# A two-layer graph kernel on one core: layer 2's attention scores as 32-row by 64-column TensorE tiles, one head in each row group, in place of keys masked by head

## The reference, cut to what matters

```python
# layer 2 (L1 in the code): 12 heads of 32 features, scale = 384 ** -0.5
q = (x @ Wq.T).reshape(b, n, 12, 32)
k = (x @ Wk.T).reshape(b, n, 12, 32)
v = (x @ Wv.T + bv).reshape(b, n, 12, 32)
bias = (adj + adj)[:, None]
scores = einsum('bqhd,bkhd->bhqk', q, k) * scale + bias
...
p = softmax(scores, axis=-1)              # a row whose scores are all zero gives zero
out = einsum('bhqk,bkhd->bqhd', p, v).reshape(b, n, h)
return out @ Wo.T + bo
# then x = layernorm(x + layer 2's result)
```

## Time and profile before

| | |
|---|---|
| median of 3 runs | 2078.02 us (2076.94 to 2078.02) |
| profiled execution, its own time | 2075.99 us |
| its span, first to last instruction | 2074.2 us |
| PE busy | 1963.2 us, 95% of the span |
| DVE busy | 1396.7 us, 67% |
| ACT busy | 1129.7 us, 54% |
| mean granted TensorE clock | 0.981 of full speed |

### The profile page before, as it was taken

One profiled execution on the slowest core, in us unless ns is written; L12 is line 12 of the kernel. 1 busy time (PEld: TensorE's weight loads), 2 busy tenths in 40 slices (PEclk: granted clock), 3 DMA queues, 4 the chain that ended last, 5 costly groups with the idle time before them and its releaser, 6 DMA issues.

```text
span 2074.2 us, 46190 instructions
## 1 busy us (share of the span) xinstructions
PE 1963.2 (95%) x16192; PEld 1878.7 (91%) x16192; DVE 1396.7 (67%) x2622; ACT 1129.7 (54%) x2456; POOL 424.9 (20%) x555
## 2 busy tenths in 40 slices
PE   5499999999999999999999999997999999999997
PEld 5399999999999999999999999997899999999997
DVE  4466666766666666766667666654777767776775
ACT  4256555565455555565555654553556565556555
POOL 2111212211121111212122121221122212221221
PEclk8699999999999999999999999999999999999999
DMA  7434444443444444444444434334222222222221
GB/s 177 125 86 119 111 114 119 108 120 102 123 112 117 108 108 130 105 116 107 115 122 107 121 101 123 104 99 116 66 83 77 66 81 83 77 67 80 84 77 63
DMA packets 268787, 213.52 MB, mean 103 GB/s; under 512 B 142928, under 2 KB 251216, under 8 KB 268752
## 3 DMA queue, kind: packets, MB, share of 16 engines
q1 hardware_dynamic: 268752, 213.06, 38.5%
HBM read 120.34 MB, written 79.69 MB: 96 GB/s over the span
## 4 chain that ended last, share of the span: by engine, by line
PE 75%; ACT 9%; DVE 8%; issue 5%; DMA 2%; SPq 1%; ACTq 0%; POOL 0%; POOLq 0%; DVEq 0%
PE a_bank L384 41%; PE b_bank L1173 15%; PE b_banks L1173 5%; PE b_banks L1215 4%; PE a_bank L450 3%; PE b_bank L1238 2%; ACT a_work L626 2%; PE a_bank L435 2%; PE b_banks L1225 2%; ACT L626 2%; ACT L594 2%; ACT a_work L594 1%; DVE a_hid_lo L772 1%; PE b_bank L1248 1%; DVE a_ctxt_lo L757 1%
## 5 line engine op out<-in xcount | busy, mean ns | idle before, releaser
L384 PE MATMUL a_bank<-a_x1t_hi,a_w_hi 128*128 128x256 f32 x1152 | 327.0, 284 | 8.3 <-DVE a_x1t_lo L757 8.3
L384 PE MATMUL a_bank<-a_x1t_hi,a_w_lo 128*128 128x256 f32 x1152 | 323.7, 281 | 0.0
L384 PE MATMUL a_bank<-a_x1t_lo,a_w_hi 128*128 128x256 f32 x1152 | 323.4, 281 | 0.0
L626 ACT ACTIVATE a_work<-a_bank,a_b 128x256 f32<-128x256 f32 x384 | 159.3, 465 | 225.6 <-PE a_bank L384 225.1
L384 PE MATMUL a_bank<-a_w_lo,a_hid_hi 128*128 128x384 f32 x768 | 258.2, 336 | 0.0
L384 PE MATMUL a_bank<-a_w_hi,a_hid_lo 128*128 128x384 f32 x768 | 258.1, 336 | 0.0
L384 PE MATMUL a_bank<-a_w_hi,a_hid_hi 128*128 128x384 f32 x768 | 258.1, 336 | 0.0
L384 PEld LDWEIGHTS a_bank<-a_x1t_hi,a_w_hi 128*128 128x128 f32 x1152 | 218.9, 190 | 17.4 <-DVE a_x1t_lo L757 8.8
L384 PEld LDWEIGHTS a_bank<-a_x1t_lo,a_w_hi 128*128 128x128 f32 x1152 | 220.9, 192 | 0.0
L384 PEld LDWEIGHTS a_bank<-a_x1t_hi,a_w_lo 128*128 128x128 f32 x1152 | 219.0, 190 | 0.0
L772 DVE TENSOR_TENSOR a_hid_lo<-a_work,a_hid_hi 128x512 fp32r<-128x512 f32 x192 | 130.1, 690 | 127.1 <-ACT a_hid_hi L631 127.1
(11 more groups left out here) (156 smaller groups left out, 5768.2 us busy)
## 6 DMA issues: line engine op xcount, KB each, us to landing
a_work<-in_x SPq DMA_DIRECT2D x64, 384.0 KB, 3.2
p_turned<-a_work SPq DMA_DIRECT2D x256, 64.0 KB, 1.8
a_work<-p_turned SPq DMA_DIRECT2D x32, 512.0 KB, 3.2
a_work<-in_xT SPq DMA_DIRECT2D x32, 384.0 KB, 3.9
ctx_turned<-a_work SPq DMA_DIRECT2D x256, 48.0 KB, 1.7
a_work<-ctx_turned SPq DMA_DIRECT2D x32, 384.0 KB, 3.1
x_turned<-a_work SPq DMA_DIRECT2D x256, 48.0 KB, 1.7
a_work<-x_turned SPq DMA_DIRECT2D x32, 384.0 KB, 3.7
```

Of the source, the lines that this page charges most:

```text
L384: r = pe.matmul(out, lhs[a], rhs[b], start=first and n == 0, stop=last and n == 2)
L626: r = act.activation(silu[:, p % 2, s * GROUP:(s + 1) * GROUP], A[p % 3][:, s * GROUP:(s + 1) * GROUP], ACT.Silu, bias=b1[:, m:m + 1])
```

## The change

- q and k of a group are copied from PSUM into one tensor `qk_t` of six blocks, without a mask: three instructions of 512 elements (`take_q(g, 0)` and `take_q(g, 1)` on ACT, `take_k` on DVE), each of which multiplies by the square root of half the score scale. The masked copies, the mask tensor and its load are gone.
- A scores matmul takes 32 rows (the features of one head), 64 weight columns (queries) and 64 moving columns (keys). There are 2 tiles x 3 blocks x 4 row groups x 2 graphs = 48 of them in a step, in the order tile, block, row group, graph. The heads of row group i of both tiles go to bank i of a four-bank PSUM tensor `four`; `two[0]` and `two[1]` are now the halves of that tensor.
- `scores(g)` is one function for both tiles: it waits for `pt_done` of both, and signals `s_mm` once, after the last matmul of both tiles.
- `soften` becomes `add_adj` (a tensor_tensor add of PSUM and adj, since the scale is in q and k already) and `find_max`. DVE's order becomes `add_adj(g, 0)`, `find_max(g, 0)`, `add_adj(g, 1)`, then `ctxt_low(g-1)` twice, then `find_max(g, 1)`.
- `attn_out(g-1, 0)` waits for `biased` of both tiles, and `turn_p(g, 0)` too.

```diff
             def scores(g, back):
+                pe.wait_ge(q_done, 2 * (g + 1))
+                pe.wait_ge(k_done, g + 1)
...
-                    pe.wait_ge(pt_done, TILES * (g - 1) + t + 1)
-                for k in range(KT):
-                    b0, b1_, h = SPAN1[k]
-                    for s in range(2):
-                        n = TILES * t + s
-                        r = pe.matmul(two[t][64 * s:64 * s + 64, h * NODES:(h + b1_ - b0) * NODES],
-                                      q[:, k, n * NODES:(n + 1) * NODES],
-                                      k_blocks[:, n, b0:b1_, :].rearrange("p b n -> p (b n)"),
-                                      start=True, stop=True, skip_group_check=True)
+                    pe.wait_ge(pt_done, TILES * g)
+                for t in range(TILES):
+                    for k in range(KT):
+                        for i in range(ROWS):
+                            row = slice(32 * i, 32 * i + 32)
+                            for s in range(2):
+                                nodes = slice((TILES * t + s) * NODES, (TILES * t + s + 1) * NODES)
+                                at = (KT * t + k) * NODES
+                                r = pe.matmul(four[64 * s:64 * s + 64, i, at:at + NODES], qk_t[row, k, nodes],
+                                              qk_t[row, KT + k, nodes], start=True, stop=True, skip_group_check=True)
                 r.then_inc(s_mm, 1)
...
             def attn_out(g, t, front):
                 pe.wait_ge(ctxt_lo, TILES * g + t + 1)
-                if front:
-                    pe.wait_ge(biased, TILES * (g + 1) + t + 1)
+                if front and t == 0:
+                    pe.wait_ge(biased, TILES * (g + 2))
...
             def take_q(g, u):
-                if u == 0:
-                    act.activation(q[:, 0:2, :].rearrange("p k n -> p (k n)"), bank[:], ACT.Copy).then_inc(q_done, 1)
-                    return
-                act.activation(q[:, 2, :], bank[:, 0:GROUP], ACT.Copy)
-                for b in range(*SPAN1[0][:2]):
-                    r = act.activation(k_blocks[:, :, b, :], bank[:, GROUP:2 * GROUP].rearrange("p (g n) -> p g n", g=GB),
-                                       ACT.Copy, scale=mask[:, b:b + 1])
-                r.then_inc(q_done, 1)
+                act.activation(qk_t[:, 2 * u:2 * u + 2, :].rearrange("p k n -> p (k n)"), one[QK_BANK[u]][:], ACT.Copy,
+                               scale=QK_SCALE).then_inc(q_done, 1)
...
             def take_k(g):
-                for k in (1, 2):
-                    b0, b1_, _h = SPAN1[k]
-                    wide_k = [P, GB, b1_ - b0, NODES]
-                    r = dve.tensor_tensor(
...
-                r.then_inc(k_done, 1)
+                dve.tensor_scalar(qk_t[:, 4:6, :].rearrange("p k n -> p (k n)"), one[QK_BANK[2]][:], QK_SCALE, None,
+                                  ALU.mult).then_inc(k_done, 1)
...
-            def soften(g, t):
+            def add_adj(g, t):
...
                 if t == 0:
+                    dve.wait_ge(s_mm, g + 1)
                     dve.wait_ge(adj_loaded, 16 * (g + 1))
                 wait(dve, shifted, TILES * (g - 1) + t + 1)
+                dve.tensor_tensor(score[:, t, :].rearrange("p (k i n) -> p k i n", k=KT, i=ROWS),
+                                  four[:, :, S // ROWS * t:S // ROWS * (t + 1)].rearrange("p i (k n) -> p k i n", k=KT),
+                                  adj_in[:, t, :].unsqueeze(1).unsqueeze(1).broadcast_to([P, KT, ROWS, NODES]),
+                                  ALU.add).then_inc(biased, 1)
+            def find_max(g, t):
...
                 if front:
-                    soften(g, 0)
+                    add_adj(g, 0)
+                    find_max(g, 0)
+                    add_adj(g, 1)
                 if back:
                     for t in range(TILES):
                         ctxt_low(b, t)
                 if front:
-                    soften(g, 1)
+                    find_max(g, 1)
```

More of the change, by code:

```diff
@@ L62 @@
 BLOCKS0, SPAN0 = head_blocks(H0)
-BLOCKS1, SPAN1 = head_blocks(H1)
-NB0, NB1 = len(BLOCKS0), len(BLOCKS1)
+BLOCKS1, _ = head_blocks(H1)
+NB0 = len(BLOCKS0)
 def wait(eng, sem, value):
@@ L197, in layer0 @@
         N_EARLY = 3 + 2
-        N_CONST = len(rows) - 1 + 3 + 2
+        N_CONST = len(rows) - 1 + 2 + 2
         last = {}
@@ L273, in load_consts @@
                         load_row(rows[name], name, const_loaded)
-                for dst, name in ((shared["mask"], "mask1"), (b1, "b1"), (shared["ident"], "ident")):
+                for dst, name in ((b1, "b1"), (shared["ident"], "ident")):
                     sp.dma_start(dst[:], w[name]).then_inc(const_loaded, 16)
@@ L1064, in layer1 @@
     S = H1 * NODES
+    ROWS = P // DH1
+    QK_SCALE = (0.5 * SCALE1) ** 0.5
     with ExitStack() as ctx:
@@ L1069, in layer1 @@
         one = [ctx.enter_context(nc.psum_tensor(f"b_bank{i}", [P, 512], F32)) for i in range(4)]
-        two = [ctx.enter_context(nc.psum_tensor(f"b_banks{i}", [P, 1024], F32)) for i in range(2)]
+        four = ctx.enter_context(nc.psum_tensor("b_banks", [P, 4, 512], F32))
+        two = [four[:, 2 * t:2 * t + 2, :].rearrange("p b c -> p (b c)") for t in range(TILES)]
         QK_BANK = (1, 0, 2)
@@ L1074, in layer1 @@
         W = {n: shared["W"][n.lower()] for n in ("Wq", "Wk", "Wv", "Wo")}
-        ident, mask = shared["ident"], shared["mask"]
+        ident = shared["ident"]
         half, eps_ln, bv = shared["half"], shared["eps_ln"], shared["bv"]
@@ L1201, in values, with scores @@
                 r.then_inc(v_mm, 1)
[L1203 to L1206, removed]
+            def scores(g, back):
+                pe.wait_ge(q_done, 2 * (g + 1))
+                pe.wait_ge(k_done, g + 1)
                 if not back:
@@ L1273, in step @@
                 if front:
-                    for t in range(TILES):
-                        scores(g, t, back)
+                    scores(g, back)
                 if back:
@@ L1306, in take_q @@
             def take_q(g, u):
-                wait(act, s_mm, TILES * g)
+                wait(act, s_mm, g)
                 act.wait_ge(qk_mm, 3 * g + u + 1)
-                bank = one[QK_BANK[u]]
-                if u == 0:
-                    act.activation(q[:, 0:2, :].rearrange("p k n -> p (k n)"), bank[:], ACT.Copy).then_inc(q_done, 1)
-                    return
-                act.activation(q[:, 2, :], bank[:, 0:GROUP], ACT.Copy)
-                for b in range(*SPAN1[0][:2]):
-                    r = act.activation(k_blocks[:, :, b, :], bank[:, GROUP:2 * GROUP].rearrange("p (g n) -> p g n", g=GB),
-                                       ACT.Copy, scale=mask[:, b:b + 1])
-                r.then_inc(q_done, 1)
+                act.activation(qk_t[:, 2 * u:2 * u + 2, :].rearrange("p k n -> p (k n)"), one[QK_BANK[u]][:], ACT.Copy,
+                               scale=QK_SCALE).then_inc(q_done, 1)
             def keep_v(g, t):
@@ L1406, in take_k @@
                 dve.wait_ge(qk_mm, 3 * g + 3)
-                wait(dve, s_mm, TILES * g)
-                for k in (1, 2):
-                    b0, b1_, _h = SPAN1[k]
-                    wide_k = [P, GB, b1_ - b0, NODES]
-                    r = dve.tensor_tensor(
-                        k_blocks[:, :, b0:b1_, :],
-                        one[QK_BANK[2]][:, (k - 1) * GROUP:k * GROUP].rearrange("p (g n) -> p g n", g=GB).unsqueeze(2).broadcast_to(wide_k),
-                        mask[:, b0:b1_].unsqueeze(1).unsqueeze(3).broadcast_to(wide_k), ALU.mult)
-                r.then_inc(k_done, 1)
+                wait(dve, s_mm, g)
+                dve.tensor_scalar(qk_t[:, 4:6, :].rearrange("p k n -> p (k n)"), one[QK_BANK[2]][:], QK_SCALE, None,
+                                  ALU.mult).then_inc(k_done, 1)
             def take_v(g, t):
@@ L1423, in take_v @@
                                   bv[:].rearrange("p (h r d) -> p h r d", r=2, d=DH1), ALU.add).then_inc(v_done, 1)
-            def soften(g, t):
-                s = score[:, t, :].rearrange("p (h n) -> p h n", h=H1)
-                dve.wait_ge(s_mm, TILES * g + t + 1)
+            def add_adj(g, t):
                 if t == 0:
+                    dve.wait_ge(s_mm, g + 1)
                     dve.wait_ge(adj_loaded, 16 * (g + 1))
                 wait(dve, shifted, TILES * (g - 1) + t + 1)
-                dve.scalar_tensor_tensor(out=s, in0=two[t][:, 0:S].rearrange("p (h n) -> p h n", h=H1), scalar=0.5 * SCALE1,
-                                         in1=adj_in[:, t, :].unsqueeze(1).broadcast_to([P, H1, NODES]),
-                                         op0=ALU.mult, op1=ALU.add).then_inc(biased, 1)
+                dve.tensor_tensor(score[:, t, :].rearrange("p (k i n) -> p k i n", k=KT, i=ROWS),
[3 more added lines that the diff above has]
+            def find_max(g, t):
                 dve.wait_ge(biased, TILES * g + t + 1)
-                dve.tensor_reduce(smax[:, t, :], s, AX_X, ALU.max).then_inc(maxed, 1)
```

(6 more changed lines are left out.)

5 lines of the change are left out of this document (3 added, 2 removed).

## The result

| | before | after |
|---|---|---|
| median of 5 runs, same chip | 2076.94 us (2074.69 to 2078.02) | 2088.07 us (2086.60 to 2088.40) |
| ratio | | 1.0055, 95% interval 1.004 to 1.0069 |
| profiled execution, its span | 2074.2 us | 2086.6 us |

The change makes the kernel 0.55% slower, about 11 us. 2086.8 us was forecast, from a median of three runs of the kernel before that stood 1.1 us above the one of five runs here. The page of the changed kernel: PE's busy time fell from 95 to 93% of the span.

A forecast was written before the change was run, and what follows sets the result against it. PE, busy 95% of the span, was taken as the bound. Steps +11.1, start -1.8 and tail -0.5 summed to +8.8 us on a median of 2078.02: 2086.8 us, own range 2083 to 2092, stated range 2080 to 2106.

The forecast's parts named there:

- D, the scores after: Length of a step's scores on PE after the change: 1.3 us, without effect on the sum if under 2.18.
- the estimate of 0.84: Scores on PE: 0.84 us, from the Trainium skill's 3.07 times the speed for four row tiles of 32 rows.
- The switch of tile shape: On PE between pv and the scores: a new change of tile shape, taken to add 0.1 us.
- The rival without sharing: Scores on PE: row groups don't share time, scores take 2.59 or 2.92 us, total 2101 or 2112 us; chance 0.15.
- DVE's string sets the step: Loop: the second add delays `ctxt_low` and so `attn_out`; each full step 0.37 us longer, +11.1 us in 30.
- `take_k` and the copies are free in the loop: Loop, DVE and ACT: shorter copies buy nothing, including 1.8 us less of DVE, since both engines wait there anyway.
- One sign in the profile: Loop, DVE: the profile after would show DVE idle before `take_k` for over 4 us.
- The start, -1.8: Start of layer 2: `take_k(0)` on the chain falls from 2.36 to 0.60 us, gaining 1.8 us.
- The tail, -0.5: Last step with a front: `find_magnitude`, on the chain, would start at 2054.6 instead of 2055.11, gaining 0.5 us.
- The clock in the loop: Loop, PE: a possible error, the clock falling because PE now pauses in each step; no size given.
- The cheap add: DVE's two adds: a rival with 0.48 us instead of 0.95 each, step 0.97 shorter, about 2047 us; chance 0.05.
- a price for reading across four banks: DVE's adds: a possible error, a PSUM read across four banks costing more than across two; no size given.

The follow-up runs named there:

- row_groups_in_turn: The changed kernel with the row group as outermost loop of the scores, so 24 records in a row go to one row group; 2100.0 us.
- order_only: The changed kernel with DVE doing both adds, then both `ctxt_low`, then both `find_max`; 2057.3 us.
- coupled_waits_old_tiles: The kernel before, with its masked 256-column scores, but with the changed kernel's signals and DVE order; 2104.2 us.
- gap_48_bytes: The changed kernel with an unused tensor of the old mask's size in its old place, restoring addresses behind it; 2086.1 us.
- copies_back: The changed kernel with the work of the removed masked copies repeated as dead work into an unused tensor; 2091.8 us.

## Why the prediction was right

Point by point, by its own steps. Sizes are from the two profiled executions, which are 12.4 us apart (the medians 11.1). That the forecast of 2086.8 us came within 1.3 us of the measured 2088.07 is in part luck: the forecast change was 8.8 us and the measured one 11.1, and 1.1 us of the difference is hidden by the higher median that the forecast started from.

- **D, the scores after.** Taken as 1.3 us between 0.65 and 2.92; measured 1.20 in the chain. Under 2.18, so it fell out of the sum, as said (with the handoff of 0.19 us the limit is 2.0). That 1.3 was so near is luck, and it made no difference; the estimate of 0.84 was too low. The switch of tile shape costs the 0.1 us assumed: from the last record of pv to the first of the scores it is 149 ns, 51 before. The rival without sharing is what row_groups_in_turn shows when one forces it.
- **DVE's string sets the step, +0.37 us, 11.1 in all.** The mechanism is shown from both sides: order_only takes one instruction out of the string and gains 31 us, coupled_waits_old_tiles has the order without the tiles and loses. The size was short: 0.48 a step, 14.3 in 30. By the chains, from pv to the end of `attn_out` it is 1721.42 - 1710.80 = 10.62 us against 1717.62 - 1707.42 = 10.20, so 0.42 of it lie where I put 0.37. What was not in the sum at all is the price of 48 bytes of shifted addresses under every full-width matmul, 0.12 us a step by gap_48_bytes. With the gap put back the step is 19.23, 0.36 over before, where the sum said 0.37.
- **`take_k` and the copies are free in the loop.** Right (copies_back: 0.01 us a step). `take_k` takes 0.69 us, I had 0.60. One sign in the profile came out otherwise: DVE idles 3.44 us before `take_k`, not over 4 (before 3.05); the time that became free lies behind it, 2.39 us of idle time before `take_v` where there were 0.63.
- **The start, -1.8.** From the first q/k matmul of layer 2 to pv of step 1: 26.42 us before, 24.59 after, -1.83. That it matches so closely is in part luck. copies_back, at nearly the clock of the changed kernel, prices the copies at 2.46 us. And between the two kernels more differs than the copies: from 1455 to 1465 us, under the first q/k matmuls, the granted clock is 0.77 before and 0.88 after, and `take_k(0)` has left the chain, which now runs over what ACT, POOL and DVE still do for layer 1. Layer 1 ended 0.4 us earlier, which nothing in the change explains (the granted clock from 1410 to 1440 us is 0.89 before, 0.94 after); over the twelve traces that point lies anywhere between 1452.8 and 1456.4 us.
- **The tail, -0.5.** Wrong in sign: from pv of step 31 to the end 27.12 before, 27.46 after, +0.3. The term itself was sound: `find_magnitude` starts 0.67 us earlier after pv, forecast 0.5. But it isn't on the chain any more, `attn_out` is. What failed is that I counted a wait as a wait only. In step 31, which has no q/k work to put in between, PE waits 2.57 us for `ctxt_low`; from 2065.3 to 2068.6 us the granted clock is 0.54, the lower of its two levels (1.2 GHz, not 2.4) nearly throughout, and the matmuls of `attn_out` start 0.32 us apart instead of 0.17. The first line is the kernel before, where the same wait is 0.84 us long and the clock stays at 1.00:

```profile
2052.93 0.44 PE L1173 MATMUL b_banks<-wo_hi,b_ctxt_hi 128*128 128x384 f32 x1 [0.84 <-DVE b_ctxt_lo L1460]
...
2065.31 0.69 PE L1175 MATMUL b_banks<-wo_hi,b_ctxt_hi 128*128 128x384 f32 x1 [2.57 <-DVE b_ctxt_lo L1454]
2065.80 0.52 PE L1175 MATMUL b_banks<-wo_hi,b_ctxt_lo 128*128 128x384 f32 x1
2066.11 0.52 PE L1175 MATMUL b_banks<-wo_lo,b_ctxt_hi 128*128 128x384 f32 x1
```

  The stretches of those 3.3 us and the 2.2 us behind them (PE, PEld, DVE, ACT, POOL busy, granted clock, DMA share, GB/s):

```profile
2065.30:2068.60 3.30, 3.29 (x11) 3.29 (x12) 3.00 (x4) 1.65 (x3) 1.93 (x2) 0.54 0.37 127
2068.80:2071.00 2.20, 2.10 (x15) 1.86 (x14) 1.24 (x6) 0.41 (x2) 0.00 (x0) 1.00 0.00 0
```

  In the chain that `attn_out` is 4.80 us long, not 3.44. Without these 1.4 us the tail would be 1.0 us shorter than before, an estimate. The other runs bear it out: in all seven kernels in which PE waits 2.56 to 2.63 us at this place the clock falls (0.50 to 0.68 over the next 3.3 us), coupled_waits_old_tiles with its old tiles among them, and `attn_out` is slow; in the five in which it waits 0.84 to 1.58 us it isn't.
- **The clock in the loop.** Named as a way to be wrong, it didn't come: between 1480 and 2060 us the granted clock is 1.00 before and after, though PE now pauses in each step.
- **The cheap add.** An add of PSUM and adj takes 0.95 us, as the scaled one; that rival is out, and so is a price for reading across four banks.

The sum of what the rows show: 14.3 - 1.8 + 0.3 - 0.4 = 12.4 us. The forecast of 8.8 had the mechanism and the sign; its largest error is the step's 0.11 us.

## What to carry to other kernels

Before making a bound engine faster, add up the next engine's string between the same two handoffs: here DVE had `ctxt_low` ready at 1713.72, 0.77 us before PE came for it at 1714.49, and the change put an instruction of 0.86 us into that string for the sake of PE's. Shared banks couple what was separate (one signal for two tiles, two adds ahead of the work that PE waits for), and that coupling ate all of the 1.4 us of saved matmul; an order that puts only what the bound engine waits for in front turned the same change into a gain. When work is moved between VectorE and GpSimd, look for VectorE instructions with two SBUF operands in the same stretch, however short.

## What the runs showed of the hardware

- Tiles of 32 rows by 64 columns: 96 records in 1.20 us when neighbours alternate over four row groups and two column halves, in 2.45 us when the row group changes only three times.
- A DVE instruction of 12 elements a partition with both operands in SBUF took 1.63 us instead of 0.17 beside POOL's 1.81 us subtraction; with one operand in PSUM it took 0.17.
- A shift of operand addresses by 48 bytes made streamed float32r matmuls of 384 columns start 175 ns apart instead of 173, and pieces of 36 matmuls last 4.28 us instead of 4.24. Which operand it is was not tried.
- A DVE add behind three waits of which the first is late started 0.18 to 0.19 us after the matmul's end in the kernel's loop, and 0.02 to 0.04 us after it in the last step, outside the loop, with the same three waits.
- In step 31 the granted clock was 0.50 to 0.68 over the 3.3 us behind PE's wait in the seven kernels where that wait was 2.56 to 2.63 us long, which cost the changed kernel 1.4 us, and 1.00 in the five where it was 0.84 to 1.58 us.
